# Attention batch steps reordered, scores in padded f32 groups, pivot columns on POOL, triangles by 63 DMAs

## The reference

```python
ada = silu(c) @ W_ada + b_ada                      # c: 16x144, six vectors of 144 per sequence
h = modulate(layernorm(x), shift_msa, scale_msa)
qkv = h @ W_qkv + b_qkv
attn = softmax((q * 9**-0.5) @ k.T)                # 16 heads of 9
x = x + gate_msa * ((attn @ v) @ W_proj + b_proj)
h = modulate(layernorm(x), shift_mlp, scale_mlp)
x = x + gate_mlp * (gelu(h @ W_fc1 + b_fc1) @ W_fc2 + b_fc2)   # hidden width 576
U, _ = qr(P)                                       # P: 144x64
v = silu(cond) @ W.T + b                           # 16 x 2016
A = zeros(16, 64, 64); A[:, iu, ju] = v; A[:, ju, iu] = -v
R = expm(A)
z = x @ U
out = x + (z @ R - z) @ U.T
```

## Time and profile before

| | |
|---|---|
| median of 3 runs | 364.18 us (362.12 to 364.23) |
| the profiled execution | 363.15 us |
| its span in the profile | 361.4 us |
| mean granted TensorE clock, share of full | 0.948 |
| PE busy | 318.2 us (88%) |
| DVE busy | 256.6 us (71%) |
| ACT busy | 187.2 us (52%) |
| POOL busy | 146.2 us (40%) |

### The profile page before, as it was taken

One profiled execution on the slowest core, in us unless ns is written; L12 is line 12 of the kernel. 1 busy time (PEld: TensorE's weight loads), 2 busy tenths in 40 slices (PEclk: granted clock), 3 DMA queues, 4 the chain that ended last, 5 costly groups with the idle time before them and its releaser, 6 DMA issues.

```text
span 361.4 us, 10608 instructions
## 1 busy us (share of the span) xinstructions
PE 318.2 (88%) x3935; PEld 245.4 (68%) x3935; DVE 256.6 (71%) x1063; ACT 187.2 (52%) x403; POOL 146.2 (40%) x421
## 2 busy tenths in 40 slices
PE   0598989889989899999999999999987957999995
PEld 0472668567877788787778777777776643467784
DVE  7381036688899989887786878988988576664243
ACT  1222464347766557567685676776762233623221
POOL 3512124235355454553543535545543508720000
PEclk9998765769999999999999999999999899999999
DMA  8817000000000000000000000000000000000013
GB/s 198 233 19 261 4 1 2 3 1 2 2 3 2 2 5 3 2 2 3 2 3 2 5 2 2 0 5 0 2 3 3 2 3 0 2 0 2 0 34 100
DMA packets 8765, 8.28 MB, mean 23 GB/s; under 512 B 1042, under 2 KB 8312, under 8 KB 8586
## 3 DMA queue, kind: packets, MB, share of 16 engines
q1 hardware_dynamic: 8006, 6.78, 6.5%
q10 hardware_dynamic: 708, 0.83, 0.8%
HBM read 6.40 MB, written 1.20 MB: 21 GB/s over the span
## 4 chain that ended last, share of the span: by engine, by line
PE 61%; DVE 18%; ACT 8%; issue 5%; POOL 4%; DMA 2%; ACTq 1%; DVEq 0%; POOLq 0%
PE bank L1255 5%; PE bank L1492 5%; PE bank L1284 4%; PE bank L1476 3%; PE bank L1318 3%; PE bank L1171 3%; PE bank L1273 3%; PE bank L1308 3%; PE bank L1300 3%; PE bank L1244 3%; PE bank L1245 2%; PE bank L1179 2%; PE bank L1274 2%; ACT KT L626 2%; PE bank L1263 2%
## 5 line engine op out<-in xcount | busy, mean ns | idle before, releaser
L440 POOL TENSOR_TENSOR root<-rec,mhalf 128x1 f32<-128x1 f32 x64 | 34.6, 540 | 107.5 <-DVE Z L922 107.5
L984 DVE TENSOR_REDUCE nmax<-bank 128x4 f32<-128x512 f32 x64 | 43.0, 672 | 34.5 <-PE bank L1263 34.2
L616 ACT ACTIVATE E<-bank 128x512 f32<-128x512 f32 x64 | 38.0, 594 | 40.6 <-PE bank L1274 40.2
L626 ACT ACTIVATE KT<-bank 64x512 bf16<-64x512 bf16 x64 | 37.5, 587 | 0.8
L1273 PE MATMUL bank<-QT,KT 128*128 128x128 bf16 x256 | 36.7, 224 | 0.0
L1274 PE MATMUL bank<-NMT,headsel 128*128 128x128 bf16 x256 | 36.3, 222 | 0.0
L1308 PE MATMUL bank<-Z,sel 128*128 128x128 f32 x128 | 29.5, 314 | 6.9 <-DVE Z L928 6.8
L1284 PE MATMUL bank<-E,V 128*32 128x128 f32 x512 | 27.9, 291 | 5.4 <-ACT E L616 5.4
L622 ACT ACTIVATE QT<-bank 128x512 bf16<-128x512 bf16 x32 | 19.0, 595 | 26.1 <-PE bank L1255 26.0
L1273 PEld LDWEIGHTS bank<-QT,KT 128*128 128x128 bf16 x256 | 24.3, 99 | 10.0 <-issue 10.0
L1308 PEld LDWEIGHTS bank<-Z,sel 128*128 128x128 f32 x128 | 20.9, 200 | 14.7 <-issue 13.6
(11 more groups left out here) (270 smaller groups left out, 827.5 us busy)
## 6 DMA issues: line engine op xcount, KB each, us to landing
gates<-gates_dram SPq DMA_DIRECT2D x1, 2304.0 KB, 8.4
x_all<-in_x_dram SPq DMA_DIRECT2D x4, 288.0 KB, 7.6
out_dram<-x_all SPq DMA_DIRECT2D x8, 144.0 KB, 2.0
wskew<-in_L_cond_W_dram SPq DMA_DIRECT2D x4, 283.5 KB
wada<-in_L_cond_W_ada_dram ACTq DMA_DIRECT2D x1, 432.0 KB
wfc1a<-in_L_cond_W_fc_dram SPq DMA_DIRECT2D x1, 288.0 KB
wfc2a<-in_L_cond_W_fc_dram SPq DMA_DIRECT2D x1, 288.0 KB
wproj<-in_L_cond_W_proj_dram SPq DMA_DIRECT2D x16, 5.1 KB
```

The lines of the kernel that those rows point to most:

```text
L440: link(nc.gpsimd.tensor_tensor(root[:, at], rec[:, at], mhalf[:, 0:1], ALU.pow))
L616: nc.scalar.activation(E[:, q, :, :].rearrange("p i t -> p (i t)"), bank[4][:, :], ACT.Exp).then_inc(s_E, 1)
L626: nc.scalar.activation(KT[parity][n][own, p, :, :].rearrange("p g t -> p (g t)"), bank[2][own, 256:512].bitcast(BF16), ACT.Copy).then_inc( ...
L984: nc.vector.tensor_reduce(nmax[:, q % 2, 4 * (q // 2):4 * (q // 2) + 4], bank[3][:, :].rearrange("p (i m) -> p i m", i=4), AX.X, ALU.max, ...
```

## The change

The generator work moves: `windows` and its 126 matmuls are gone, and SP issues 63 DMAs from `v` in SBUF to `A0` in SBUF, each for one row of every triangle; `triangles` masks the result in place at b = 4. The entries of v are computed in batch steps 0 and 1, and the stages of the exponential stand five batch steps later than before (`ENTRIES` to `SQUARE`), the squarings at b = 12 to 15. The front is reordered: the condition and the first modulations come first, the transposes of W after queries and keys of sequence 0. Three elimination steps are done ahead of the batch steps, and every fifth batch step has three instead of four (`STEPS`).

The scores become f32: four heads are laid side by side in slots of 32 columns (`qstk`, `kstk`, `SL = 32`), and four row groups of 32 partitions each make 8 matmuls with 128 columns for 8 heads into four banks. There are two such groups in a batch step instead of four. The negated maximum is written into column 9 of the query stack against a column of ones in the key stack, and the query stack is transposed again (`queries_again_T`), so that the transposed scores come out with the maximum subtracted; `maxima_parts`, `headsel`, `rest` and `low` are gone. The sums come out of a column of ones in V; `sums`, `division` and `reciprocal_sums` are gone, and outputs are transposed back (`heads_back`), divided over 144 columns and transposed again (`normalized_T`) for a projection of two matmuls. ACT exponentiates 1024 columns at a time, twice.

In each elimination step the three column operations `c`, `cB` (the sign) and `w` leave DVE; DVE copies the pivot column to `bk`, POOL computes `sgn`, `c` and `w` (`pivots`), and DVE waits for them (`s_piv`) ahead of its reciprocal. `sel` is gone: the stationary operand is a column of the identity read with stride 0.

```diff
 def eliminations(k, ...):
     ...
     if G:
         got_rec = lk.mark(nc.vector.reciprocal(rec[:, kk], bank[7][:, kk]))
     if B:
-        wait(dve, s_zm, k)
-        got_c = lk.mark(STT(c[:, :], bkk, cG[:, j], zm[:, :], ALU.mult, ALU.subtract))
-        wait(dve, s_root, k)
-        got_sign = lk.mark(TS(cB[:, :], bkk, 0.0, nroot2[:, j], ALU.is_ge, ALU.mult))
+        nc.vector.tensor_copy(bk[:, j], bank[7][:, jp]).then_inc(s_bk, 1)
     if G:
         lk.need(got_rec)
         got_cG = lk.mark(TS(cG[:, kk], Z[:, kk], rec[:, kk], negmask[:, kk], ALU.mult, ALU.mult))
-    if B:
-        lk.need(got_sign)
-        got_pivot = lk.mark(STT(w[:, :], cB[:, :], root[:, j], bkk, ALU.add, ALU.subtract))
     if G:
         lk.need(got_cG)
         STT(Z[:, 0:2 * RD], bank[7][:, 0:2 * RD], cG[:, kk], Z[:, 0:2 * RD],
             ALU.mult, ALU.add).then_inc(s_Gstep, 1)
     if B:
-        lk.need(got_pivot)
-        link(nc.vector.reciprocal(w[:, :], w[:, :]))
-        link(STT(cB[:, :], c[:, :], w[:, :], cG[:, j], ALU.mult, ALU.add))
+        dve.wait_ge(s_piv, k)
+        link(nc.vector.reciprocal(wi[:, :], w[:, j]))
+        link(STT(cB[:, :], c[:, j], wi[:, :], cG[:, j], ALU.mult, ALU.add))
         STT(Z[:, 2 * RD:3 * RD], bank[7][:, 2 * RD:3 * RD], cB[:, :], Z[:, 2 * RD:3 * RD],
             ALU.mult, ALU.add).then_inc(s_Bstep, 1)
...
+def pivots(k):
+    at = slice(k - 1, k)
+    pool.wait_ge(s_bk, k)
+    pool.wait_ge(s_root, k)
+    pool.wait_ge(s_zm, k)
+    link(nc.gpsimd.tensor_scalar(sgn[:, at], bk[:, at], 0.0, nroot2[:, at], ALU.is_ge, ALU.mult))
+    lk.mark(nc.gpsimd.tensor_scalar(c[:, at], bk[:, at], cG[:, at], zm[:, :], ALU.mult, ALU.subtract))
+    done = lk.n
+    nc.gpsimd.tensor_scalar(w[:, at], sgn[:, at], root[:, at], bk[:, at], ALU.add, ALU.subtract).then_inc(s_piv, 1)
+    lk.need(done)
...
+for i in range(RD - 1):
+    at = (RD - 1) * i - i * (i - 1) // 2 - i
+    sp.wait_ge(s_v, min(4, (at + RD - 2) // 504 + 1))
+    sp.dma_start(A0[i:i + RD + 1:RD, :, :], v[:, at:at + RD]).then_inc(s_win, 16)
...
+def stack_T(dst, stack, done):
+    for j in range(4):
+        ins = pe.transpose(dst[:, 128 * j:128 * j + 128], stack[:, 4 * j:4 * j + 4, :].rearrange("p h s -> p (h s)"),
+                           ident[:, :])
+    ins.then_inc(done, 1)
...
+def scores(b, g):
+    ...
+    for j in range(2):
+        for r in range(4):
+            rows = slice(32 * r, 32 * r + 32)
+            ins = mm(bank[r][:, 128 * j:128 * j + 128], QT[rows, 2 * g + j, :], KT[b % 3][rows, 2 * g + j, :],
+                     start=True, stop=True)
+    ins.then_inc(s_S, 1)
...
+def maximum(b, g):
+    dve.wait_ge(s_S, 2 * b + g + 1)
+    wait(dve, s_qmT, b - 1)
+    nc.vector.tensor_reduce(qstk[b % 2][:, 8 * g:8 * g + 8, D:D + 1].rearrange("p (j r) a -> p r (j a)", r=4),
+                            scored(g).rearrange("p r (j m) -> p r j m", j=2),
+                            AX.X, ALU.max, negate=True).then_inc(s_max, 1)
...
+def exponentials(b, g):
+    act.wait_ge(s_ST, 2 * b + g + 1)
+    wait(act, s_pv, 2 * b - 1 + g)
+    nc.scalar.activation(E[:, g, :, :, :].rearrange("p r j t -> p r (j t)"), scored(g), ACT.Exp).then_inc(s_E, 1)
```

1254 lines of the change are left out of this document (658 added, 596 removed).

## The result

The changed kernel takes 365.4 us (median of 14 runs, 363.77 to 366.79), the kernel before 362.23 (14 runs, 360.43 to 364.23). The ratio is 1.009, with a 95% interval of 1.007 to 1.012: no gain, where 327 was forecast.

A forecast was written before the change was run, and what follows sets the result against it. DVE and PE together were taken to bound a late batch step, DVE a little more. From 363.15 us, 16.6 less in the sixteen batch steps, 16 in the front and 3.5 in batch steps 16 and 17 gave 327; range 302 to 350.

The forecast's parts named there:

- the trip over POOL: Each elimination: sending sign, `c` and `w` to POOL makes it 1.85 us instead of 1.53, 0.32 more, with DVE idle 0.4.
- the clock falls: Rival, chance 0.07: PE does less and waits more, so its clock drops; with twelve such batch steps 382 us.
- What is late next: DVE waits for row copies, 1.0 us in quarter 1 and 0.6 in quarter 3, making a late batch step 12.5 us.
- The quarter 3 wait: DVE's wait for row copies in quarter 3: the normalization covers 0.25 of 0.8 us, leaving 0.6.
- a hidden trip: Rival, chance 0.21: `sgn`, `c` and `w` take 0.7 us together, all behind the update of G; 307 us.
- the loop gains nothing: Rival, chance 0.13: unseen waits for row copies take 1.0 us of each batch step, only front and end gain; 344 us.
- the factor of 3.07: Skill's speedup of four row tiles over one; by it a score group takes 0.13 us more, the sum 4 us higher.
- the front: Stretch before batch step 0: moved entries, windows and exponential let batch step 0 start at 31 us, 16 less.
- the score groups: PE's scores: eight f32 matmuls of 128 columns in row groups take 0.57 us, four groups in a batch step 2.3.
- the 63 DMAs: SP's small transfers, 0.36 us each: the last 32 issued by 67 us, needed at 97; free up to 1.2 each.
- Batch steps 16 and 17: Last two batch steps lose two sums, divisions and reciprocals and part of a root: 3.5 of 20.0 us (1 to 6).
- the signs by which the prediction would be known wrong: POOL operations outside 0.2 to 0.35 us; PE or ACT releasing DVE's maxima over 1 us a batch step; loop clock below 0.9.

## Why the prediction was wrong

**The step that failed is the trip over POOL.** The forecast had the sign at 0.26, a pause of 0.10, and `w` "some 0.2 behind" `c`, "since it doesn't wait for `c`"; DVE's reciprocal at 1.24. Measured: 0.31, a pause of 0.11, 0.36 from `c` to `w`, 0.37 for `w`, and the reciprocal at 1.50. An elimination takes 2.15, not 1.85. POOL starts the next of these operations only when the one ahead of it is nearly done, waiting or not, and `c` and `w`, which read two columns beside their input, take 0.37 to 0.38, where the two of the earlier trace rows, with one such column at most, take 0.26 and 0.27. I had given the upper end (2.2) in the text as a bound and then taken a value near the lower rows. By size this term isn't the largest that failed: the accounting at the end of this section gives it 6 us net of the 38, the lower clock that came with it 13 to 14, and what else the loop needs some 15.

The same arithmetic took VectorE 0.11 to 0.13 us from start to start in the kernel without the trip, and POOL 0.36 to 0.42 here: three times as long. The Trainium skill, "GPSIMD Engine Reference", Section 3.1, has a reason that fits: two software hops for each instruction on GPSIMD where VectorE has one. It gives no figure for GPSIMD's hops; the trace agrees with the direction, and the size is the trace's alone. That the hops are the cause no run here shows.

**The rival "the clock falls" was half right, and I had made it exclusive.** It had 0.07, as a world in which everything else goes well. In fact the longer trip and the lower clock come together: while DVE waits for POOL, TensorE waits for DVE. The matched batch steps, cut at the projection of queries, keys and values show what the trip costs by itself where both kernels are at full clock; the changed kernel's batch steps 4, 5, 9 and 12 at full clock, and 13 at 0.89:

```profile
99.85:111.88 12.03, 10.18 (x138) 7.32 (x135) 7.79 (x26) 6.11 (x13) 6.55 (x20) 1.00 0.01 2
111.88:126.34 14.46, 11.63 (x174) 8.82 (x170) 9.90 (x38) 5.99 (x13) 8.72 (x26) 1.00 0.00 1
175.49:188.08 12.59, 11.33 (x171) 8.39 (x167) 9.82 (x32) 6.71 (x14) 7.16 (x20) 1.00 0.01 3
223.53:238.45 14.92, 12.64 (x207) 9.78 (x203) 9.42 (x37) 7.07 (x15) 9.62 (x28) 1.00 0.01 2
238.45:254.23 15.78, 14.12 (x206) 11.02 (x202) 9.31 (x36) 7.08 (x15) 8.34 (x26) 0.89 0.01 2
```

and the same five without the trip, all at full clock:

```profile
86.12:96.88 10.76, 10.15 (x139) 7.33 (x135) 8.59 (x36) 6.00 (x13) 3.63 (x11) 1.00 0.01 2
96.88:109.37 12.49, 11.55 (x174) 8.82 (x171) 10.13 (x46) 5.99 (x13) 4.54 (x14) 1.00 0.01 1
151.12:162.46 11.34, 11.18 (x171) 8.36 (x167) 10.71 (x39) 6.59 (x14) 4.51 (x12) 1.00 0.01 4
190.93:204.52 13.59, 12.56 (x206) 9.78 (x203) 9.74 (x44) 7.08 (x15) 5.35 (x16) 1.00 0.00 1
204.52:218.11 13.59, 12.55 (x206) 9.78 (x202) 9.62 (x44) 7.08 (x15) 4.09 (x14) 1.00 0.01 3
```

The first four differences are 1.27, 1.97, 1.25 and 1.33. Batch steps 4 and 9 have three eliminations, 5 has four, and 12 has four and a squaring. In units of 0.62 that is about 2, 3, 2 and 2: the length of one trip in each batch step is covered, and of a second one in a batch step with a squaring. By the kernels with trips in one quarter alone, quarter 2 costs its full length in all four, and quarter 0 costs 0.1 to 0.25 in batch steps 4, 5 and 12; in batch step 9 it costs 0.59, so there it is quarter 1 that is covered. In batch steps 12 to 14, with a squaring, the wait in quarter 2 is 0.98 in the changed kernel and 1.60 without the trip: the trip of quarter 1 fits into it, since TensorE's two products stand in the queue there. So about 61 - 16 - 4 = 41 trips count, 25 us, an estimate from four batch steps.

The loop differs by 38.9; the other 13 or 14 would then lie in the batch steps in which the changed kernel is at a lower clock. The last row of each view gives a price for that: batch steps 12 and 13 are equally long without the trip, and in the changed kernel 13 takes 0.86 us more at a clock of 0.89, which is 1.7 us of clock lost (0.11 x 15.78). In the kernel with trips in quarter 2, 13 takes 1.60 more than 12, 15.83 for 14.23, also at 0.89. The changed kernel's loop loses 30 us of clock (0.12 x 250.25) and the loop without the trip 6 (0.03 x 211.28): 24 more, by these two prices 12 to 22 us, an estimate that holds the 13 to 14. That the 13 to 14 us are the clock's alone is worked out and not shown by a run of its own; that the lost clock costs over 6 is shown.

**"What is late next" had the right number and left out a queue.** It had 1.0 us of waiting in quarter 1, from two transposes and the handovers, and the changed kernel has 0.94 to 0.95 in plain batch steps (241.62). Without the trip it is 1.33 to 2.0, since the projection and the transposed scores stand in TensorE's queue ahead of the row copies; in the changed kernel the trip of quarter 0 covers that. That PE's 9.6 us a batch step are "covered by DVE" is true of the sum and not of this stretch. The quarter 3 wait was right (0.6 forecast, 0.55 measured). By the same sum, a kernel with a hidden trip should take 307; the one without the trip takes 323 to 331. So even with an elimination priced at 1.53 the forecast would have been 16 to 24 us too low, 15 of it in the loop (211.3 for 196) of the profiled run. This queue and the clock are part of it. The rival "the loop gains nothing" named the kind of wait and had 0.13 of the chance. One sum of the prediction is off, without a bearing on the forecast: by the factor of 3.07 that it names, eight matmuls of 0.29 take 0.76, which is 0.19 above 0.57 and not 0.13, and 6 us in all and not 4. The group took 0.65, between the two.

**Right were** the front (30.6 for 31), the back (62.5 for 62.4), the maximum of 1024 columns (1.13 from start to start, two in 2.3), the wait of quarter 3, the score groups (0.65 for 0.57), and the 63 DMAs: issued from 39.9 to 81.5 us, masked at 109.7, without a wait. Batch steps 16 and 17 took 20.3 for 16.5, at a clock of 0.50; without the trip 17.0. Two of the signs by which the prediction would be known wrong came: POOL operations above 0.35 and a clock below 0.9 in the loop (0.88).

**In the 38 us** between 327 and 365, then: the longer trip, 0.30 in 41 eliminations that count, 12; in 20 eliminations the forecast counted 0.32 that is covered, 6 back; the lower clock in the loop, 13 to 14; the 15 us by which the loop without the trip stands above the sum; and 4 in batch steps 16 and 17, which are at half clock. How the 15 split into TensorE's queue, the clock and woven work, no run here shows.
